# Local-attention layer of an eight-part fused network: the order of a phase rewritten on four engines

## What is computed

```python
def attn_layer(x, Wqkv, qs, ksc, Wo):
    q, k, v = split(x @ Wqkv)            # 16 heads of 64
    q = l2norm(q) * qs;  k = l2norm(k) * ksc
    q = rotate(q, cos * scale);  k = rotate(k, cos / scale)
    sim = einsum(q, own and previous window of k) * 8    # windows of 32 tokens
    attn = softmax(where(mask, -big, sim))
    return (attn @ v) @ Wo

for i in range(6):
    x = attn_layer(shift_tokens(x), ...) + x
    x = ffn_layer(shift_tokens(x), ...) + x   # layernorm, W1, a * gelu(gate), W2
```

## Time and profile before

| | |
|---|---|
| time, median of 3 runs | 9594.64 us (9582.53 to 9597.06) |
| the profiled execution, its own time | 9595.29 us |
| its span | 9593.5 us |
| mean granted clock of TensorE over the span | 0.841 |
| PE busy over the span | 7189.6 us, 75% |
| DVE / ACT / POOL busy | 6310.2 / 3257.3 / 3567.5 us (66, 34, 37%) |
| DMA queues, share of 16 engines | 7.7% for data |
| PE in the chain that ended last | 27% of the span |

### The profile page before, as it was taken

One profiled execution on the slowest core, in us unless ns is written; L12 is line 12 of the kernel. 1 busy time (PEld: TensorE's weight loads), 2 busy tenths in 40 slices (PEclk: granted clock), 3 DMA queues, 4 the chain that ended last, 5 costly groups with the idle time before them and its releaser, 6 DMA issues. The chain is left out here.

```text
span 9593.5 us, 242768 instructions
## 1 busy us (share of the span) xinstructions
PE 7189.6 (75%) x91413; PEld 4409.5 (46%) x91543; DVE 6310.2 (66%) x13775; ACT 3257.3 (34%) x5970; POOL 3567.5 (37%) x4941
## 2 busy tenths in 40 slices
PE   4777777877774637457746678888888888888887
PEld 2666666666622222233223244444544445454544
DVE  7555555555557665855584567777777777777776
ACT  2222222222242313223413334444444444444444
POOL 1555555545400000300040045555555555555553
PEclk7888888778887767657765789999999999999999
DMA  0000000000000000000000121111111111111111
GB/s 18 1 1 1 1 1 1 1 1 1 0 5 0 14 0 0 0 1 1 0 0 1 41 89 51 55 51 48 55 49 56 51 54 52 48 52 52 51 55 57
DMA packets 156953, 243.03 MB, mean 25 GB/s; under 512 B 21616, under 2 KB 136848, under 8 KB 150160
## 3 DMA queue, kind: packets, MB, share of 16 engines
q1 hardware_dynamic: 155920, 228.84, 7.7%
HBM read 187.06 MB, written 13.66 MB: 21 GB/s over the span
## 5 line engine op out<-in xcount | busy, mean ns | idle before, releaser
L2656 POOL TENSOR_TENSOR big<-big 128x512 f32<-128x512 f32 x388 | 494.6, 1275 | 1920.0 <-DVE big L2498 1920.0
L2666 POOL TENSOR_TENSOR big<-big 128x512 f32<-128x512 f32 x776 | 1045.7, 1380 | 241.2 <-DMA big<-norms 233.6
L1771 POOL TENSOR_TENSOR small<-big 128x480 f32<-128x480 f32 (+14 forms) x240 | 220.8, 954 | 2192.1 <-ACT big L1529 1872.1
L587 ACT ACTIVATE big<-big 128x128 f32<-128x128 f32 x1024 | 317.1, 310 | 1872.2 <-DVE big L735 1782.2
L2073 PE MATMUL banks<-hidden,big 128*128 128x256 f32 x3104 | 837.6, 404 | 111.9 <-DVE big L2498 41.5
L798 POOL TENSOR_TENSOR big<-big 128x128 f32<-128x128 f32 x1024 | 467.1, 456 | 1220.4 <-DVE big L747 1055.5
L498 PE MATMUL banks<-big,constants_on_chip 128*128 128x128 f32 x2048 | 572.1, 367 | 411.6 <-DVE big L739 407.6
L335 PE MATMUL banks<-big,weights_even 128*128 128x512 f32 (+5 forms) x1152 | 623.0, 694 | 234.3 <-DVE big L1052 45.1
L335 PE MATMUL banks<-big,constants_on_chip 128*128 128x512 f32 (+15 forms) x1088 | 526.1, 636 | 361.1 <-DVE big L1662 191.9
L2116 PEld LDWEIGHTS banks<-big 32*32 32x32 f32 x49152 | 545.4, 104 | 513.2 <-issue 512.7
L2137 PE MATMUL banks<-big,hidden 128*32 128x512 f32 x6144 | 776.8, 600 | 4.4 <-ACT big L2388 4.1
(11 more groups left out here) (348 smaller groups left out, 15293.7 us busy)
## 6 DMA issues: line engine op xcount, KB each, us to landing
big<-norms SPq DMA_DIRECT2D x776, 128.0 KB, 2.9
big<-qk SPq DMA_DIRECT2D x50, 512.0 KB, 4.6
big<-vo SPq DMA_DIRECT2D x25, 1024.0 KB, 6.0
weights_odd<-ffn SPq DMA_DIRECT2D x25, 537.5 KB, 5.6
hidden<-big SPq DMA_DIRECT2D x171, 64.0 KB, 4.2
hidden<-big SPq DMA_DIRECT2D x25, 256.0 KB, 3.5
hidden<-big SPq DMA_DIRECT2D x25, 255.8 KB, 4.2
big<-pairs SPq DMA_DIRECT2D x6, 1024.0 KB, 10.7
```

Source lines behind the costliest of these rows:

```text
L2656: self.nc.gpsimd.tensor_tensor(dst, cos, sin, ALU.add).then_inc(*e.did(("turned_pair", f, name, g)))
L2666: self.nc.gpsimd.tensor_tensor(x, x, u["norms"][:, n, g].unsqueeze(1).broadcast_to([P, 2, QTOK]), ALU.mult).then_inc(*e.did(("scaled", f, ...
```

## The change

What it does, all inside the local layer:
- PE: `score_masks(f, 0)` and the first half's scores move to the head of the phase (masks directly behind K projections 0 to 2). `attend(f - 1, 1)` moves behind two of these scores. The second half's scores, values and Q projections are mixed differently, and `attend(f, 0)` stands before the last two windows of scores. `mean` moves from the end of phase 0 into phase 1.
- DVE: `lower(f, 0)` comes ahead of the query ropes and `normalise(f, 0)` between query ropes 1 and 2. `normalise(f, 1)` moves into the next phase, behind the first rope. The gates and norms follow the query guard.
- ACT: `exps(f, 1)` moves into the next phase, `exps(f, 0)` ahead of the inverse of the keys; the gelus of a phase share one pair of table loads.
- POOL: key scaling goes ahead of the last two query adds. SP is untouched.
- `entry` clears five slots and `prob[1]` and no longer `probT[1]`; `exit` does the last `exps` and `normalise`.

No arithmetic in the loop is added or dropped, apart from two ACT table loads (each way) fewer per phase 2 and 3.

```diff
 local_tensor
         for f in range(QUARTERS):
             for g in range(3):
                 t.project(f, "K", g)
+            t.score_masks(f, 0)
+            t.score(f, 0, 0)
+            t.project(f, "K", 3)
+            t.score(f, 0, 1)
             t.attend((f - 1) % QUARTERS, 1)
-            t.project(f, "K", 3)
+            t.score(f, 0, 2)
+            t.turn_back(f)
+            if f == 1:
+                t.mean(0)
             t.value(f, 0, 0)
+            t.score(f, 0, 3)
+            if f == 1:
+                t.mean(1)
             t.value(f, 0, 1)
             t.sums(f, "K")
             t.project(f, "Q", 0)
-            t.score_masks(f, 0)
-            t.score(f, 0, 0)
+            t.value(f, 0, 2)
             t.project(f, "Q", 1)
-            t.score(f, 0, 1)
-            t.turn_back(f)
+            t.value(f, 0, 3)
+            t.score_masks(f, 1)
+            t.score(f, 1, 0)
             t.project(f, "Q", 2)
-            t.score(f, 0, 2)
             t.project(f, "Q", 3)
-            t.score(f, 0, 3)
+            t.value(f, 1, 0)
+            t.score(f, 1, 1)
             t.sums(f, "Q")
-            t.value(f, 0, 2)
-            t.value(f, 0, 3)
+            t.value(f, 1, 1)
+            t.attend(f, 0)
...
+            t.score(f, 1, 2)
...
+            t.value(f, 1, 2)
...
+            t.score(f, 1, 3)
+            t.value(f, 1, 3)
             if f >= 2:
                 t.down(f - 2)
 local_vector
+            v.rope(f, "K", 0)
+            v.normalise((f - 1) % QUARTERS, 1)
+            for g in range(1, GROUPS):
+                v.rope(f, "K", g)
             v.add(f, (turn % BATCH) * SEQ + (f - 1) * QTOK if f else old + 3 * QTOK)
             if f == 1:
+                v.centre(0)
+            v.lower(f, 0)
+            if f == 1:
+                v.centre(1)
+            v.guard(f, "K")
+            v.rope(f, "Q", 0)
+            v.rope(f, "Q", 1)
+            v.normalise(f, 0)
+            v.rope(f, "Q", 2)
+            v.rope(f, "Q", 3)
+            v.guard(f, "Q")
 local_scalar
+            a.square(f, "K", 0)
+            a.exps((f - 1) % QUARTERS, 1)
+            for g in range(1, GROUPS):
                 a.square(f, "K", g)
+            a.attention(f)
             a.keep_value(f, 0, 0)
             a.keep_value(f, 0, 1)
+            a.exps(f, 0)
             a.inverse(f, "K")
...
+            a.square(f, "Q", 0)
...
+            a.square(f, "Q", 2)
+            a.square(f, "Q", 3)
+            a.keep_value(f, 1, 0)
             a.inverse(f, "Q")
+            a.keep_value(f, 1, 1)
 local_pool
+            for g in range(GROUPS):
+                p.add(f, "K", g)
+            p.add(f, "Q", 0)
+            p.add(f, "Q", 1)
             p.keep_last(f)
+            for g in range(GROUPS):
+                p.scale(f, "K", g)
+            p.add(f, "Q", 2)
+            p.add(f, "Q", 3)
+            for g in range(GROUPS):
+                p.scale(f, "Q", g)
```

More of the change, by code:

```diff
@@ L2143, in attend @@
         e, pe, u = self.e, self.pe, self.u
+        pe.wait_ge(*e.after("turned", q, jj))
         if e.layer == "local":
-            kw = {"back": 1} if jj and q == QUARTERS - 1 else {}
-            pe.wait_ge(*e.after("turned", q, jj, **kw))
-            pe.wait_ge(*e.after("kept", q, jj, 3, **kw))
+            pe.wait_ge(*e.after("kept", q, jj, 3, **({"back": 1} if jj and q == QUARTERS - 1 else {})))
             if jj == 0:
@@ L2278, in entry_vector @@
         e.name_last("folded", d, "vector")
+    for k in range(2 * (SUBS * QUARTERS) - 5, 2 * (SUBS * QUARTERS)):
+        nc.vector.memset(u["slots"][k % SLOTS], 0.0).then_inc(*e.did())
+    dve.wait_ge(*e.after("stored", DEPTH - 1))
+    nc.vector.memset(u["prob"][1].rearrange("p c k -> p (c k)"), 0.0).then_inc(*e.did())
     e.leave()
@@ L2307, in local_tensor @@
             t.project(f, "Q", 0)
-            t.score_masks(f, 0)
-            t.score(f, 0, 0)
+            t.value(f, 0, 2)
             t.project(f, "Q", 1)
-            t.score(f, 0, 1)
-            t.turn_back(f)
+            t.value(f, 0, 3)
+            t.score_masks(f, 1)
+            t.score(f, 1, 0)
             t.project(f, "Q", 2)
-            t.score(f, 0, 2)
             t.project(f, "Q", 3)
-            t.score(f, 0, 3)
+            t.value(f, 1, 0)
+            t.score(f, 1, 1)
             t.sums(f, "Q")
-            t.value(f, 0, 2)
-            t.value(f, 0, 3)
+            t.value(f, 1, 1)
+            t.attend(f, 0)
             if f == 1:
                 t.variance(0)
[L2322 to L2325, removed]
             if f >= 2:
                 t.up(f - 2, 0)
[L2328 to L2339, removed]
+            t.score(f, 1, 2)
+            if f == 1:
+                t.variance(1)
+            if f >= 2:
+                t.up(f - 2, 1)
+            t.value(f, 1, 2)
+            if f >= 2:
+                t.up(f - 2, 2)
+            t.score(f, 1, 3)
+            t.value(f, 1, 3)
             if f >= 2:
@@ L2374, in exps @@
         e, act = self.e, self.act
-        act.wait_ge(*e.after("lowered", f, jj))
+        if e.layer == "local":
+            act.wait_ge(*e.after("lowered", f, jj, **({"back": 1} if jj and f == QUARTERS - 1 else {})))
         p = self.u["prob"][jj].rearrange("p c k -> p (c k)")
@@ L2414, in ffn_inverse, with gelus @@
             *e.did(("frstd", h)))
-    def gelus(self, h, ks):
+    def gelus(self, h):
         e, act = self.e, self.act
         self.nc.scalar.preload_act_table(ACT.Gelu)
-        for k in ks:
+        for k in range(len(IC)):
             n = IC[k][1]
@@ L2445, in local_scalar @@
                 a.ffn_squares(0)
+            a.square(f, "Q", 0)
+            if f == 1:
                 a.ffn_squares(1)
[L2447 to L2448 removed]
             a.keep_value(f, 0, 2)
+            a.square(f, "Q", 1)
             a.keep_value(f, 0, 3)
+            a.square(f, "Q", 2)
+            a.square(f, "Q", 3)
+            a.keep_value(f, 1, 0)
             a.inverse(f, "Q")
+            a.keep_value(f, 1, 1)
             if f == 1:
@@ L2726, in exit_scalar @@
     for h in range(HALVES):
-        a.gelus(h, range(3))
+        a.gelus(h)
     core.to_act.restart("out")
@@ L2736, in exit_vector @@
     start = (BATCH - 1) * SEQ
+    v.normalise(QUARTERS - 1, 1)
     v.add(0, start + 3 * QTOK)
```

54 lines of the change are left out of this document (11 added, 43 removed).

## The result

The changed kernel takes **9685.17 us** (median of 4 runs, 9678.64 to 9688.35) against 9595.85 us for the kernel before on the same chip (4 runs, 9582.53 to 9597.13): a ratio of 1.0092, 95% interval 1.0080 to 1.0104. It is slower by 0.9%. The forecast was 9680.

The account below looks back on a forecast made before the run. A 37.3 us query-reply loop from masks to masks was to bound phases 0 and 1, PE phase 2; with added terms, phases of 42.5, 41.2, 41.8 and 41.9 made 167.4 us a turn, 82 us over 24, plus 3: 9680 (9460 to 9830).

Parts of the forecast that it names:

- The longest loop of waits afterwards: From masks to masks through softmax, query norms, DMA and POOL's query scaling: 37.3 us a phase.
- step 6: SP and DMA, from issue of the outgoing query norms to the first scaling: 6.4 us, plus 2.7 in phase 0.
- step 7: POOL's four query scalings: 5.4 us, between 4.95 and 5.87, or 5.7 with the handoffs at either end.
- 5.87 throughout: By the skill's contention rule, query scaling beside normalise(f, 1) takes 5.87 us in every phase, adding about 1 us a turn.
- Late attend and loop edge in phase 0: Half 1's attend waits for its softmax, plus 1.5 us; DVE stands before its first rope, plus 1.0.
- The clock in phases 1 and 2: PE at granted clock 0.50 behind the masks' waits: plus 2.0 us in each phase, between 0 and 5.0.
- The rival of 5.0 for each: Low clock through the whole head: 5.0 us lost behind the masks' waits in phases 1 and 2, 9826 us; chance 0.15.
- Issue stalls in phases 2 and 3: PE stalls inside the scores with nothing to wait for: plus 1.0 us in phase 2 and 1.6 in phase 3.
- Attend waits: PE's waits before the attends for the transpose ending a softmax shrink from 11.7 us a turn to about 3.
- The reply is not the bound: Rival: queries are ready and PE's own work bounds, 24 x 14 us less, 9260 us; chance 0.06.
- Cheap ends: Rival: same loop, no clock fall, cheaper terms, 156 us a turn, 9410 us, or 9542 with half; chance 0.21.
- gains and losses meet: Rival: the new wait is as long as the old ones, 9595 us within 0.2%; chance 0.09.

Follow-up runs that it names:

- Experiment 9: Changed kernel with POOL's four query scalings removed, the masks waiting for the last query add instead: 9357.71 us, ratio 0.9737 to the kernel before.
- Experiment 7: Changed kernel with useless matmuls ahead of the masks' wait for the query scaling, 36 in phase 1 and 24 in phase 2: 9592.72 us, ratio 0.9990.
- experiment 2: Kernel before with the outgoing query norms sent twice, one extra DMA trip before the reply: 9512.33 us, ratio 0.9906.
- experiment 8: Kernel before with the second norm of phase 1 moved from ahead of lower(1, 1) to behind normalise(1, 1): 9530.74 us, ratio 0.9923.

## Why the prediction was right, step by step

**What bounds it: right.** "The longest loop of waits afterwards" was to be the query reply in phases 0 and 1, PE in 2 and 3. Experiment 9 takes the reply out and shortens just phases 0 and 1. For phase 3 it is shown that the reply is not the bound, not that PE is.

**The turn: right, by terms that partly cancelled.** Phases forecast and measured:

| phase | forecast | measured in the turn shown | mean of 22 turns |
|---|---|---|---|
| 0 | 42.5 | 42.4 | 42.1 |
| 1 | 41.2 | 40.8 | 42.1 |
| 2 | 41.8 | 40.5 | 40.1 |
| 3 | 41.9 | 43.1 | 42.9 |
| turn | 167.4 | 166.8 | 167.2 |

That the sum is right to 0.2 us is luck in part: each phase is off by 0.4 to 1.7 us, and single terms by up to 2.6 us.

- *Query reply, step 6: mis-sized both ways.* I took 6.4 us from norms out to scaling, and 9.1 in phase 0. Measured in this turn's timeline: 7.7 in phase 0 (7129.17 to 7136.89), 7.2 in phase 1 (7170.46 to 7177.69); over all turns 7.4 and 7.8. Phase 0's slow trip was not a property of SP's program in that place; it was worth +1.0, not +2.7, and phase 1 had +1.4 that I did not give it.

```profile
7129.17 0.51 SPq L1975 DMA_DIRECT2D norms<-weights_even  x1
...
7170.46 0.52 SPq L1975 DMA_DIRECT2D norms<-weights_even  x1
```

```profile
7136.89 4.94 POOL L2673 TENSOR_TENSOR big<-big 128x512 f32<-128x512 f32 x4 [4.08 <-DMA big<-norms]
...
7177.69 4.94 POOL L2673 TENSOR_TENSOR big<-big 128x512 f32<-128x512 f32 x4 [4.24 <-DMA big<-norms]
```

- *POOL's scaling, step 7: right in the mean, 5.4, but not in each phase.* The turn shown has 4.94 in both phases, the low end. Over all turns it is 5.14 in phase 0 and 5.79 in phase 1, where 19 of 22 lie above 5.5; in phases 2 and 3 it is 4.95. Phase 1 of an earlier turn shows what lies beside the slow ones, the product of the normalise:

```profile
6007.72 5.92 POOL L2673 TENSOR_TENSOR big<-big 128x512 f32<-128x512 f32 x4 [4.60 <-DMA big<-norms]
...
6011.14 1.37 DVE L2541 TENSOR_TENSOR big<-big,heads 128x1024 f32<-128x1024 f32 x1
```

  Where it overlaps POOL's scalings by more than 0.3 us, this product takes 1.56 us in the mean (32 times), elsewhere 1.23 (160 times). The Trainium skill (GPSIMD Engine Reference, Specifications) has POOL contend with two-input instructions of VectorE. The trace agrees where the two meet, and both engines pay; the sum by it, 5.87 throughout, is borne out in phase 1 only, since in phase 0 the product is mostly done before the scaling starts (7135.61 to 7136.83, and 7136.89 in the turn shown), and in phases 2 and 3 they don't meet. In the kernel before, the norms met POOL: 3.0 us for 1.2 us of norms, and 5.87 for 4.95 of scaling, which the prediction had among its rows and did not ask about.
- *Late attend and loop edge in phase 0: 4.4 us for 2.5.* The attend of half 1 starts 2.21 us after PE was ready, and 0.98 us of waiting for a bank lies ahead of it. Behind these is DVE, which stands 3.44 us before the first rope of a turn, where the earlier trace rows had 1.96. And the clock fell there too, which the prediction had in phases 1 and 2 only: 64 matmuls in 3.14 us (3.04 in the mean of 23 turns), 1.2 more than the 1.95 of the earlier trace rows.

```profile
7100.12 0.48 DVE L2501 SCALAR_TENSOR_TENSOR big<-banks,heads,big 128x256 f32<-128x256 f32 x1 [3.44 <-ACT big L2384]
...
7105.96 3.14 PE L2154 MATMUL banks<-big 128*32 128x128 f32 x64 [2.21 <-DVE big L2547]
```

- *The clock in phases 1 and 2: right.* Waits of 8.56 and 5.51 us are followed by 0.50. The pieces behind cost 0.44 + 0.32 + 0.94 + 0.32 + 0.08 more than at full clock, 2.1 us, where I took 2.0, and the attend itself is nearly at full speed. Experiment 7 priced it from the other side, 3.9 us a turn for both. The rival of 5.0 for each had the mechanism right and its length wrong. The Trainium skill (TensorE: Matmul & The Clock Gate, "HAM oscillation") warns of this pattern. With these rows it is right on the fall; taken fully, its sum of 9824 is 139 us too dear.
- *Issue stalls in phases 2 and 3, plus 2.6 a turn: wrong.* All 4.9 us a turn vanished. Phase 2 is 1.7 us shorter in the mean than forecast, and 1.0 of that was this term. Why the stalls went is open. The scores may no longer run beside SP's large transfers: SP issues these behind the query norms, and in the new order PE waits at the masks then. The busy share of the DMA engines while scores run without a stall (every fourth such window) did fall, from 0.34 to 0.12, and in experiment 2 the trip delays SP, the stalls halve, and those left stand at a share of 0.71 against 0.30. But in the kernel before, the share is 0.37 in the 64 longest stalls and 0.34 outside, so there the traffic alone doesn't tell them apart.
- *Phase 3, 42.9 for 41.9,* takes back part of what phase 2 gave, and 1.6 us of stalls that were in the forecast are not in it either: some 2.6 us were not foreseen. In experiment 9 it is 42.1 with no query scaling at all, so most of it isn't the reply. Part is the clock again: the late attend there takes 2.71 us in the mean for 1.95, behind a wait of 2.1. Which of gelu, gate or `down` sets the rest was not tried.
- *Attend waits: near,* 100.6 us in 23 turns or 4.4 a turn, against "about 3".

**The rivals.** "The reply is not the bound" (9260) is out: removing it gives 9357.71. "Cheap ends" needed the clock not to fall. Where it is kept from falling in phases 1 and 2, experiment 7 shows the result, 9593: the time of "gains and losses meet", almost exactly.

**What I did not foresee** is that the kernel before held a removable 71 us in one wait. The prediction read that chain as the softmax's own length.

## What to carry to other kernels

When scores and softmax of a half are pulled apart, the work that fills the gap is paid by the next reply in the round: follow the whole loop from a wait back to itself, and add its pieces, for each phase of its own. The PE waits of 5 to 9 us at the masks cost 2 us of half clock each on top of themselves; filling them with matmuls that nobody reads was worth as much (92 us) as the change lost. And before reordering around a long wait, look at whether an instruction in its chain runs slow beside another engine: one layer norm moved by a step gave 0.8%, without any of the rest.

## What the runs showed of the hardware

- DVE beside POOL: mean of 24 over two milliseconds, first before, then experiment 8. Alone they take 0.71 and 0.49 us (experiment 2), beside POOL's scaling 1.62 and 1.38. TENSOR_SCALAR slows 2.8 times, SCALAR_TENSOR_TENSOR 2.3 times. POOL pays as well: its four scalings take 4.97 us in the mean alone, and 5.8 where the norms or the product of the normalise overlap them by 1 us or more. In experiment 8 only one of the two norms still meets POOL. Columns: group and count, busy us, mean ns, idle before.

```profile
L2568 DVE SCALAR_TENSOR_TENSOR hidden<-hidden,weights_odd 128x512 f32<-128x512 f32 x24 | 37.0, 1542 | 5.7 <-ACT hidden L2413 5.7
...
L2571 DVE TENSOR_SCALAR hidden<-hidden,weights_odd 128x512 f32<-128x512 f32 x24 | 33.3, 1388 | 0.8
```

```profile
L2568 DVE SCALAR_TENSOR_TENSOR hidden<-hidden,weights_odd 128x512 f32<-128x512 f32 x24 | 24.9, 1039 | 5.7 <-ACT hidden L2413 5.7
...
L2571 DVE TENSOR_SCALAR hidden<-hidden,weights_odd 128x512 f32<-128x512 f32 x24 | 22.6, 940 | 0.9
```

- A delay can be a gain: one more trip to DRAM in every phase made the kernel before 0.9% faster.
- PE at half clock is not half as fast for every shape: 64 matmuls of 32 x 32 take 1.11 us instead of 0.79, a projection of 128 x 128 2.00 instead of 1.06, and a wait of only 2.2 us, 0.98 us of waiting a little ahead of it, is followed by an attend of 3.04 us in the mean of 23 turns, while the 2.3 us around did nothing in the kernel before.
- The same DMA of query norms from SBUF to DRAM took 3.10 us in phase 0 and 2.64 in phase 1 of one turn; from its issue to the scaling it was 6.7 to 8.1 us in phase 0 and 7.2 to 8.8 in phase 1 over all turns.
